# Attention's first batch: its shift on ScalarE chunk by chunk, and the first scores ahead of the value tiles

## What is computed

```python
scale, shift = jnp.split(emb @ W_emb + b_emb, 2, axis=-1)
xn = _rms_norm(x, g_norm) * (1.0 + scale) + shift
q, k, v = split_heads(xn @ W_qkv)
q = _rms_norm(q, g_q)                       # over each head's 32 features
k = _rms_norm(k, g_k)
attn = softmax(einsum('bhqd,bhkd->bhqk', q, k) * d ** -0.5)
o = merge_heads(einsum('bhqk,bhkd->bhqd', attn, v))
x = x + o + o @ W_out
...
x = x + gru(cond, x)                        # 512 steps, one after the other
x = x + causal_conv(x, cond)
x = x + causal_conv(x, cond) + b
```

## Time and profile before

| | |
|---|---|
| median of 3 runs | 2217.25 us (2214.75 to 2222.03) |
| the profiled execution | 2214.76 us, span 2212.8 us |
| mean granted TensorE clock | 0.991 of full |
| TensorE busy | 2126.4 us, 96% of the span |
| VectorE, ScalarE, GpSimd busy | 1389.0, 1186.0, 1134.9 us |
| start of the GRU's first recurrent matmul | 617.87 us |

### The profile page before, as it was taken

One profiled execution on the slowest core, in us unless ns is written; L12 is line 12 of the kernel. 1 busy time (PEld: TensorE's weight loads), 2 busy tenths in 40 slices (PEclk: granted clock), 3 DMA queues, 4 the chain that ended last, 5 costly groups with the idle time before them and its releaser, 6 DMA issues.

```text
span 2212.8 us, 184515 instructions
## 1 busy us (share of the span) xinstructions
PE 2126.4 (96%) x76736; PEld 1590.4 (72%) x76736; DVE 1389.0 (63%) x5092; ACT 1186.0 (54%) x5992; POOL 1134.9 (51%) x3895
## 2 busy tenths in 40 slices
PE   6899999999989999999999999999999999999997
PEld 1222222222379999999999999999999988888886
DVE  1444443444257777777777777777777777777775
ACT  2344444443245555555555555555555555565554
POOL 1142432433135556555555656556555666666665
PEclk9899999999999999999999999999999999999999
DMA  6000000001022222112222221122221100000000
GB/s 247 1 1 1 1 1 1 1 20 59 32 58 51 54 54 51 49 51 53 68 52 52 54 53 49 50 70 55 50 51 50 48 5 24 6 6 5 5 7 19
DMA packets 159135, 86.69 MB, mean 39 GB/s; under 512 B 126016, under 2 KB 154944, under 8 KB 158272
## 3 DMA queue, kind: packets, MB, share of 16 engines
q1 hardware_dynamic: 158896, 83.42, 14.0%
q10 hardware_dynamic: 144, 2.10, 0.2%
HBM read 26.37 MB, written 12.58 MB: 18 GB/s over the span
## 4 chain that ended last, share of the span: by engine, by line
PE 66%; DVE 4%; issue 1%; DMA 1%; POOL 0%; ACT 0%; POOLq 0%; SPq 0%; DVEq 0%
PE ps L1106 60%; PE ps L1134 6%; DVE arena L962 3%; DVE arena L979 1%; DMA arena<-arena 1%; POOL arena L1171 0%; ACT ps L1039 0%; DVE arena L968 0%; PE ps L1141 0%; DVE arena L974 0%; POOL arena L1175 0%; POOL arena L1177 0%; DVE arena L1011 0%; DVE seq L992 0%; ACT arena L1070 0%
## 5 line engine op out<-in xcount | busy, mean ns | idle before, releaser
L1106 PE MATMUL ps<-whh,arena 128*4 128x128 f32 (+1 forms) x65536 | 1452.7, 246 | 34.2 <-DVE arena L979 27.2
L1106 PEld LDWEIGHTS ps<-whh,arena 128*4 128x4 f32 x65536 | 1310.3, 87 | 157.5 <-DVE arena L979 77.9
L962 DVE STREAM_TRANSPOSE arena<-ps 128x128 f32<-128x128 f32 x1024 | 434.7, 425 | 250.0 <-PE ps L1106 249.7
L1064 ACT ACTIVATE arena<-arena 128x8 f32<-128x8 f32 x1024 | 215.6, 211 | 649.5 <-DVE arena L962 628.0
L1171 POOL TENSOR_TENSOR arena<-tap,seq 128x32 f32<-128x32 f32 x1024 | 231.5, 257 | 256.3 <-DVE seq L992 256.3
L381 DVE TENSOR_REDUCE top<-ps 128x2 f32<-128x1024 f32 x128 | 150.8, 1220 | 257.5 <-PE ps L620 257.5
L979 DVE TENSOR_TENSOR_SCAN arena<-arena 128x24 f32<-128x24 f32 x1024 | 214.6, 210 | 144.8 <-ACT arena L1075 144.8
L1039 ACT ACTIVATE ps<-arena 128x128 f32<-128x128 f32 x1026 | 269.8, 263 | 0.7 <-PE ps L1141 0.7
L1171 POOL TENSOR_TENSOR arena<-tap,arena 128x32 f32<-128x32 f32 x1024 | 231.3, 257 | 66.8 <-POOL arena L1181 66.8
L968 DVE STREAM_TRANSPOSE arena<-ps 128x64 f32<-128x64 f32 x1024 | 253.2, 247 | 10.8 <-PE ps L1106 1.5
L523 PE MATMUL ps<-arena 128*32 128x512 f32 x2048 | 246.0, 600 | 11.5 <-POOL arena L214 11.5
(11 more groups left out here) (89 smaller groups left out, 1298.9 us busy)
## 6 DMA issues: line engine op xcount, KB each, us to landing
arena<-arena SPq DMA_DIRECT2D x240, 104.0 KB, 2.1
arena<-seq SPq DMA_DIRECT2D x128, 104.0 KB, 2.1
arena<-gi_d SPq DMA_DIRECT2D x256, 32.0 KB
gi_d<-arena SPq DMA_DIRECT2D x108, 52.0 KB, 1.6
seq<-in_x SPq DMA_DIRECT2D x4, 1024.0 KB, 17.1
arena<-arena SPq DMA_DIRECT2D x32, 128.0 KB, 2.1
whh<-in_w_hh SPq DMA_DIRECT2D x1, 3072.0 KB, 21.2
arena<-seq SPq DMA_DIRECT2D x24, 128.0 KB, 2.2
```

The lines of the kernel that those rows point to most:

```text
L962: e.transpose(trn[:, h].rearrange("p q (i c s) -> p q c i s", c=2, s=2)[:, :, :, :, 0], bank[RN[h]][:, 0:P].rearrange("p (q c i) -> p q c ...
L1064: e.activation(r_d0[:, h].rearrange("p (i s) -> p i s", s=2)[:, :, 1], trn[:, h, 0, 0:2 * NH].rearrange("p (i s) -> p i s", s=2)[:, :, 0], ...
L1106: last = e.matmul(bank[dst[h]][32 * G:32 * G + B, 0:n], hv, wv[:, k, gates, G, 64 * h:64 * h + 64], start=False, stop=k2 == 1 and k == C - ...
```

## The change

ScalarE adds the first batch's shift, with an Identity activation whose bias is the shift, a chunk at a time as VectorE delivers it, in place of GpSimd. The first q projection waits for one chunk at a time. In TensorE's prologue the four value tiles move behind: `project(0, 1)` is split around `norm(1, 0)`, `scores(0, 0)` comes next, the value tiles follow among the scores, `value_tile(-1, 0)` just ahead of `turn_tops(0)` and `value_tile(-1, 1)` inside the loop at n = 0, ahead of `project(0, 2)`. The waits that guard the two PSUM banks follow that order, and `weigh(0, j)` waits for j + 1 value tiles in place of four. ScalarE's copies are reordered in the same way.

```diff
@@ gpsimd
-                add_shift(0)
                 for n in range(NS):
                     add_first(n)
@@ scalar
                 rms_x(0)
+                for c in range(C):
+                    e.wait_ge(d_xn, c + 1)
+                    e.activation(xnT[:, c], xnT[:, c], ACT.Identity, bias=modT[:, 1, c, 0:1]).then_inc(g_xn, 1)
                 keep(0, 0)
                 keep(1, 0)
-                values(-2, 0)
                 rms(0, 0)
                 rms(1, 0)
-                values(-2, 1)
                 keep(0, 1)
                 keep(1, 1)
                 rms(0, 1)
+                values(-2, 0)
+                rms(1, 1)
+                values(-2, 1)
                 values(-1, 0)
-                rms(1, 1)
-                values(-1, 1)
...
                     exponentials(n, 0)
+                    if n == 0:
+                        values(-1, 1)
@@ tensor, project
-                            if c == 0:
+                            if c == 0 and b:
                                 e.wait_ge(g_xn, C * b + C)
-                            free(e, n - 3, s, n)
+                            if n == 1:
+                                e.wait_ge(a_sq[s], 1)
+                            else:
+                                free(e, n - 3, s, n)
+                        if n == 0 and s == 0:
+                            e.wait_ge(g_xn, k + 1)
@@ tensor, value_tile
-                            e.wait_ge(a_sq[i], n + 3)
+                            if n == -1:
+                                e.wait_ge(a_v, i + 1)
+                            else:
+                                e.wait_ge(a_sq[i], max(n + 3, 2))
@@ tensor, weigh
-                    if j == 0:
+                    if n == 0:
+                        e.wait_ge(a_v, j + 1)
+                    elif j == 0:
                         e.wait_ge(a_v, TB * b + TB)
-                        if n:
-                            e.wait_ge(d_o, n)
+                        e.wait_ge(d_o, n)
@@ tensor, the prologue
                 project(0, 0, range(C))
                 project(1, 0, range(C))
-                value_tile(-2, 0, range(C))
                 e.wait_ge(d_const, 12)
                 norm(0, 0)
+                project(0, 1, range(0, 2))
                 norm(1, 0)
-                value_tile(-2, 1, range(C))
-                project(0, 1, range(C))
+                project(0, 1, range(2, C))
                 scores(0, 0)
                 project(1, 1, range(C))
                 scores(0, 1)
                 norm(0, 1)
-                value_tile(-1, 0, range(C))
+                value_tile(-2, 0, range(C))
                 scores(0, 2)
                 norm(1, 1)
-                value_tile(-1, 1, range(C))
+                value_tile(-2, 1, range(C))
                 scores(0, 3)
+                value_tile(-1, 0, range(C))
                 turn_tops(0)
...
                     shifted(n, 0)
+                    if n == 0:
+                        value_tile(-1, 1, range(C))
```

## The result

| | before | changed |
|---|---|---|
| median | 2217.01 us (2214.75 to 2222.03, 4 runs) | 2202.1 us (2199.38 to 2203.72, 4 runs) |
| ratio | | 0.9928, 95% interval 0.9909 to 0.9948 |
| profiled execution | 2214.76 us, span 2212.8 | 2203.72 us, span 2201.9 |

The forecast was 2202.8.

What follows compares the result with a forecast made beforehand. TensorE, busy for 96% of the span, was taken as the bound. 8.2 - 0.2 + 0.2 + 3.07 + 3.95 - 0.7 = 14.5 us off 2214.76 gave 2200.3, and 2.5 more for the median 2202.8; range 2197.5 to 2208.5.

Steps and rivals of the forecast that it cites:

- The start: Ahead of the first projection: it starts at 20.0 instead of 28.20, 8.2 us earlier.
- The clock behind that gap: Behind the gap ahead of the first projection: the clock falls again at about 20.8, net -0.2 us.
- Rival (a): The clock doesn't fall behind the gap ahead of the first projection: 2201.4 us; chance 0.15.
- The first scores: Ahead of the first scores: the 0.80 gap goes, one of 0.6 comes, net +0.2; scores at about 34.3.
- The gap at `turn_tops`: Ahead of group 0's transposed maxima: the value tile put there removes the 3.07 us gap.
- The slow stretch that went with it: The low clock from 68.6 to 78.8, around group 0's transposed maxima, goes: 3.95 us given back.
- rival (b): The clock falls around the gaps ahead of `shifted(0, 0)`, costing 1.4 to 2.6 us: 2204.2 to 2205.4; chance 0.2.
- `value_tile(-1, 1)` behind `shifted(0, 0)` costs nothing: In the loop at n = 0: moves 3.5 us paid in both kernels; nobody waits, so no cost.
- All of it reaches the end: From `project(0, 2)` to the end: the whole 14.5 us gained in the prologue arrives.
- (c): In the prologue: slow add, late chunks or a value tile missing its place: 2206 to 2208 us; chance 0.1.
- (d): Behind the prologue: something with its own timetable, loading, ends last and no gain arrives: 2217 us; chance 0.04.
- (e): In the prologue: the chunk-wise start feeds TensorE too thinly, clock stays at 1.2 GHz: up to 2242 us; chance 0.01.

Runs made afterwards that it cites:

- e4: The changed kernel, but the first q projection waits for all four chunks instead of one at a time; 2209.72 us, ratio 0.9946.
- e5: The changed kernel plus three products that nobody reads, right behind the input's sum of squares; 2202.86 us, ratio 0.9934.
- e1: The kernel before with only the shift moved to ScalarE, chunk by chunk, TensorE's order as it was; 2210.23 us, ratio 0.9954.
- e3: The changed kernel with `value_tile(-1, 0)` moved from ahead of `turn_tops(0)` to behind `shifted(0, 0)`; 2210.61 us, ratio 0.9954.
- e6: The changed kernel with `value_tile(-1, 1)` ahead of `shifted(0, 0)` and its copy ahead of the first exponentials; 2198.86 us, ratio 0.9917.
- e8: The changed kernel itself, measured again on another occasion; 2202.74 us, ratio 0.9932.
- e9: e7 plus one product that nobody reads in each of four gaps at the ends of groups 0 and 1; 2201.31 us, ratio 0.9918.
- e11: e7 with GpSimd's `add_third` ahead of `add_shift` in groups 1, 5 and 9; 2193.72 us, ratio 0.9881.
- e2: The changed kernel with the shift back on GpSimd and the first projection waiting for all four chunks; 2214.84 us, ratio 0.9974.
- e7: The changed kernel with the edits of e5 and e6 together; 2196.48 us, ratio 0.9905.
- e10: The kernel of e7 measured once more; 2199.24 us, ratio 0.9907.
- e12: The kernel of e7 measured a third time; 2198.59 us, ratio 0.9904.

## Why the prediction was right, by its steps

- **The start**, 8.2 us: 8.27 measured, the first projection at 19.93 for 20.0. The Identity took 0.72 for the 0.69 that I took from the Ln. Chunks came 0.67 apart and not 0.77, the first after 0.75: 3.09 / 4 was a mean over three short ones and one of 1.10. The small errors cancel. e4 shows that 2.0 of the 8.27 is the wait for single chunks.
- **The clock behind that gap**, -0.2: it fell at 20.6 for the 20.8 forecast. It stayed low for 3.4 us, and e5 sizes it at 1.70 of work where I took 1.6. By the rule of the Trainium skill, "TensorE: Matmul & The Clock Gate", Part 1, that the point of a change shifts between runs, the gap could have passed without a fall in some of them; no profile here shows that with the gap open: the clock fell behind it in the changed kernel, e1, e3, e4, e6 and e8. Rival (a) did not come. (Its price was added up wrongly: from -0.2 to +1.4 are 1.6 us, so it stood at 2201.2 and not 2201.4, and the sum at 16.1 and not 15.9. Nothing hangs on it.)
- **The first scores**: the forecast gap of 0.6 is 0.62, at 34.48 for 34.3.
- **The gap at `turn_tops`**, 3.07: gone, the row at 54.65 for about 54.7. e3 brings the gap back, and at least 2.0 us with it.
- **The slow stretch that went with it**, 3.95, and -0.7 for the gap ahead of `shifted(0, 0)`: the term that was mis-sized. The old slow stretch is gone, but the gap of 1.44 and the one in the middle of `shifted(0, 0)` brought a new one, 58.2 to 65.0, 3.4 us of work. This is rival (b), to which I gave 0.2 and a price of 1.4 to 2.6. It came in both profiles of the changed kernel, and the tile's copy and `project(0, 2)` are 3.3 us later than forecast for it, at a clock that was to be full there and was half until 65.0. e6, which closes the gap, has 3.9 us less. It should have been the likeliest case: the fall at 102.7 in the earlier trace rows came behind gaps of 0.35, 0.15 and 1.45 us, 2 us in all within a short stretch, the last of them in the timeline of the kernel before:

```profile
102.16 1.58 PE L620 MATMUL ps<-arena 32*128 32x512 f32 x8 [1.45 <-ACT arena L296]
```

- **`value_tile(-1, 1)` behind `shifted(0, 0)` costs nothing**: right for the queues, as nobody waited for ScalarE. But it is the wrong side of the gap; ahead of it, it would have been worth as much as one of my terms.
- **All of it reaches the end**: nearly so in the profile, where 11.5 us after the prologue ended as 10.9. It was not a steady 14 to 15 us on every later row, as the signs had it: the lead went to 13.1 and back, and the first recurrent matmul came at 607.17 for 603. The clock falls at the end of group 1 in every profile, in some at the end of group 0 too, and for lengths that differ: before, from 102.7 and from 136.9, 3.4 us each; changed, once, from 123.0, for 10.2.
- The forecast's median of 2202.8 was thus right by a sum that was 3.4 too high in one place in the profiled execution, 2200.3 forecast against 2203.72, and a median that lay 1.6 below that execution where the median of before lies 2.3 above its own. That part was luck: the profiles show a gain of 11, the medians one of 14.9, and what the other executions did in between isn't seen.
- Rivals (c), (d) and (e): no chunk was late, the gain did arrive, and under steady work the clock came back after 3.4 us.

## What to carry to other kernels

Read a gap on a bounding TensorE together with the granted clock behind it: here 2.0 us of waiting cost 5.4 in the profile, 3.4 of it to the clock, and the cure that paid was work that has to be done anyway, moved across the gap (e6); work that nobody reads kept the clock up where it stood, and lowered no median by itself (e5, e9). When a saving in one place doesn't reach the end, look for the next engine that keeps its own timetable: an earlier TensorE only waited longer for GpSimd (e9), until the addition that it waits for went ahead of 8.8 us of work that nobody needed yet (e11, 4.9 us). When one kernel is slower than another, compare their rows to the very end before naming the cause: in the profiles e9 falls behind ahead of the GRU, not where its edit is. And in a prologue, where most engines rest, a pass belongs to a resting engine that is quick at it: 2.2 us a chunk on GpSimd against 0.7 on ScalarE, with a wait for one chunk at a time, was worth 8.3 us.

## What was not expected of the hardware

- VectorE's scaling of the fourth chunk took 1.10 us in the kernel before, where GpSimd works on the first chunk beside it, and 0.74 in the changed kernel. Four chunks took 3.09 us there and in e2, which has GpSimd beside them too, and 2.74 in the changed kernel, e1 and e4. The Trainium skill, "GPSIMD Engine Reference", section 1 (Specifications), says that GpSimd shares its SBUF interfaces with VectorE and that they contend when VectorE's instruction has two SBUF inputs, as this one has. The rows agree for the last of the chunks; the two before it overlap GpSimd as well and took 0.75, so the rule is not the whole of it. GpSimd's own first chunk, beside VectorE's, took 2.88 us and the other three 5.92, 1.97 each.
- With the clock kept up in the first gap (e5), it was low for 10.2 us further on, between 120 and 131; the kernel differs from the changed one by twelve matmuls. It happens without the twelve too: the changed kernel's first profile has 10.2 us there and its second 3.4, and e7 and its repeats e10 and e12 have 10.2, 3.4 and 3.4. Why the same gaps cost so differently from one execution to the next stays open.
- The GRU, the same code in all of them, took from its first recurrent matmul to the span's end 1594.9 us before, 1594.7 in the changed kernel, and 1599.2 in e6, 1599.1 in e3, 1599.7 in e4. The granted clock doesn't explain it: in e3 and e4 it is at full from 3 us or so after the GRU's start on. What makes the difference of up to 5 us wasn't tried; it is a third of the change's gain, and one profile can't be read against another below it.
